# Expert slots cut to narrower widths by rank, with the largest expert in the seventh slot

## The reference

```
gating = x @ router_w.T                       # 1024 x 8
probs = softmax(gating); topk_w, sel = top_k(probs, 2)
h = x @ w1[e].T                               # per expert e: 512 -> 2 x 1024
y = h[..., 1024:] * silu(h[..., :1024])
out = sum over the two chosen experts of topk_w * (y @ w2[e].T)   # 1024 -> 512
```

## Time and profile before

| | before |
|---|---|
| median of three executions | 2489.52 us |
| the profiled execution | 2492.94 us |
| its span | 2491.2 us |
| granted clock of TensorE over the span | 0.978 |
| PE busy in the span | 2365.6 us (95%) |
| DVE, ACT, POOL busy | 51%, 44%, 45% |
| the expert stage | about 2076 to 2491 us |
| DMA in the expert stage | about 155 GB/s |

### The profile page before, as it was taken

How to read it: one execution, slowest core, us unless ns; L and a number is a source line. 1 busy time by engine, 2 the same in 40 slices (tenths; PEclk the granted TensorE clock), 3 DMA queues, 4 the chain that set the end, 5 groups by cost and what they waited for, 6 DMA issues and landing times. The chain is left out here.

```text
span 2491.2 us, 41300 instructions
## 1 busy us (share of the span) xinstructions
PE 2365.6 (95%) x14585; PEld 2088.6 (84%) x14585; DVE 1275.7 (51%) x2146; ACT 1091.7 (44%) x1866; POOL 1119.0 (45%) x470
## 2 busy tenths in 40 slices
PE   8999999999999999999999999999758986999997
PEld 6798989889898988989898898889636756999986
DVE  3255555555555555555555554555755445555542
ACT  3354544445454444445444444444422213444442
POOL 2254555555455555555555555555530014132223
PEclk9999999999999999999999999999979987999999
DMA  4311121211112121211212121111040026465443
GB/s 154 99 48 48 41 60 33 76 41 57 48 41 58 35 76 35 63 48 41 52 41 71 36 66 48 41 48 45 5 161 1 19 81 192 140 168 159 148 146 82
DMA packets 148049, 177.59 MB, mean 71 GB/s; under 512 B 83312, under 2 KB 106736, under 8 KB 147824
## 3 DMA queue, kind: packets, MB, share of 16 engines
q1 hardware_dynamic: 138112, 147.63, 19.9%
q0 software_dynamic: 5104, 10.24, 2.1%
q10 hardware_dynamic: 4608, 16.78, 2.1%
HBM read 135.12 MB, written 39.48 MB: 70 GB/s over the span
## 5 line engine op out<-in xcount | busy, mean ns | idle before, releaser
L395 POOL TENSOR_TENSOR k_parts<-k_t,k_parts 64x1602 fp32r<-64x1602 f32 x128 | 426.1, 3329 | 448.1 <-DVE k_parts L460 448.0
L716 PE MATMUL ps_kv<-ctx_hi,wk_hi 128*128 128x256 f32 (+1 forms) x1536 | 462.5, 301 | 7.6 <-DVE ctx_lo L574 7.6
L716 PE MATMUL ps_kv<-ctx_lo,wk_hi 128*128 128x256 f32 (+1 forms) x1536 | 440.4, 287 | 0.0
L716 PE MATMUL ps_kv<-ctx_hi,wk_lo 128*128 128x256 f32 (+1 forms) x1536 | 440.3, 287 | 0.0
L409 POOL TENSOR_TENSOR v_parts<-v,v_parts 128x832 fp32r<-128x832 f32 x128 | 283.2, 2213 | 335.6 <-ACT v_parts L643 334.1
L506 DVE TENSOR_TENSOR probs_t<-ps_pt,probs_t 128x512 fp32r<-128x512 f32 x368 | 205.8, 559 | 443.8 <-ACT probs_t L625 439.9
L716 PE MATMUL ps_kv<-wv_hi,ctx_hi 128*128 128x512 f32 (+1 forms) x832 | 341.5, 410 | 1.9 <-DVE wv_lo L544 1.9
L716 PE MATMUL ps_kv<-wv_hi,ctx_lo 128*128 128x512 f32 (+1 forms) x832 | 328.2, 394 | 0.0
L716 PE MATMUL ps_kv<-wv_lo,ctx_hi 128*128 128x512 f32 (+1 forms) x832 | 327.3, 393 | 0.0
L613 ACT ACTIVATE k_t<-ps_kv,bk_sb 128x256 f32<-128x256 f32 (+1 forms) x384 | 185.8, 484 | 312.3 <-PE ps_kv L716 309.6
L716 PEld LDWEIGHTS ps_kv<-ctx_hi,wk_hi 128*128 128x128 f32 x1536 | 291.3, 190 | 10.5 <-issue 8.7
(11 more groups left out here) (257 smaller groups left out, 4015.0 us busy)
## 6 DMA issues: line engine op xcount, KB each, us to landing
ctx_raw<-ctx_dram SPq DMA_DIRECT2D x81, 512.0 KB, 3.8
w_raw<-w_dram SPq DMA_DIRECT2D x64, 512.0 KB, 3.6
rows_in<-zeros SPq DMA_DIRECT2D x150, 128.0 KB, 3.5
w_raw<-w_dram ACTq DMA_DIRECT2D x32, 512.0 KB, 3.7
ctx_raw<-ctx_dram SPq DMA_DIRECT2D x16, 644.0 KB, 5.5
q_blocks<-q_parts SPq DMA_DIRECT2D x256, 32.0 KB, 2.0
rows<-rows_in SPq DMA_DIRECT2D x8, 768.0 KB, 4.7
q_parts<-probs_t SPq DMA_DIRECT2D x16, 256.0 KB, 2.0
```

The lines of the kernel that those rows point to most:

```text
L395: nc.gpsimd.tensor_tensor(k_parts[64 - 64 * s:128 - 64 * s, :], k_t[par][64 * s:64 * s + 64, g, :], k_parts[64 * s:64 * s + 64, :].bitcast ...
L716: last = nc.tensor.matmul(o, still, moving, start=(k == 0 and i == 0), stop=(k == DT - 1 and i == 2))
```

## The change

The widths by rank become 384, 320, 320, 288, 288, 256, 192 and 128. Slots are also put in another order: slots 0 to 5 hold ranks 1 to 6, slot 6 holds rank 0 (384 rows), and the last slot rank 7 (128 rows). A width is no longer a bound that always holds: rows past a slot's width go to overflow slots, whose number is counted anew (`most_extra` gives 6, so there are again three passes of the loop). Tiles are cut to the rows that are computed: a slot of 320 rows has tiles of 128, 128 and 64 rows, one of 288 has 128, 128 and 32, one of 256 two of 128, one of 192 has 128 and 64, and the last one a single tile. The counters that engines wait on count these tiles. The rows of a slot are still loaded and transposed as 384.

```diff
-WIDTH = [min(BLOCK, -(-(2 * NT // (k + 1)) // 2) * 2) for k in range(E)]
-LAST_RB = -(-WIDTH[-1] // P)
+WIDTH = [320, 320, 288, 288, 256, 192, BLOCK, 128]
+RANK_OF_SLOT = [1, 2, 3, 4, 5, 6, 0, 7]
+def tile_rows(s):
+    width = WIDTH[s] if isinstance(s, int) else BLOCK
+    return [min(P, width - r * P) for r in range(-(-width // P))]
+def tiles_before(s):
+    if isinstance(s, int):
+        return sum(len(tile_rows(k)) for k in range(s))
+    return s * RB - sum(RB - len(tile_rows(k)) for k in range(E - 1))
...
 def add_rows(s, par, tiles):
-                for r in range(tiles):
+                for r, m in enumerate(tiles):
                     nc.gpsimd.indirect_dma_start(
-                        out=out, out_offset=bass.IndirectOffsetOnAxis(ap=slot_slips[par][:, r, 0:1], axis=0),
-                        in_=down[:, r, :], in_offset=None, compute_op=ALU.add).then_inc(added, 16)
+                        out=out, out_offset=bass.IndirectOffsetOnAxis(ap=slot_slips[par][0:m, r, 0:1], axis=0),
+                        in_=down[0:m, r, :], in_offset=None, compute_op=ALU.add).then_inc(added, 16)
...
 def weigh_down(s, par, tiles):
                 if positive(s):
-                    act.wait_ge(added, 16 * RB * s)
+                    act.wait_ge(added, tiles_before(s) * 16)
...
 def down_part(s, k, tiles):
-                for r in range(tiles):
-                    yh, yl = (part[:, k, r * P:(r + 1) * P] for part in (y_hi, y_lo))
+                for r, m in enumerate(tiles):
+                    yh, yl = (part[:, k, r * P:r * P + m] for part in (y_hi, y_lo))
                     for i, (still, moving) in enumerate([(yh, w2_hi), (yh, w2_lo), (yl, w2_hi)]):
-                        last = nc.tensor.matmul(ps_d[r][:], still, moving[:, k, :], start=(k == 0 and i == 0),
+                        last = nc.tensor.matmul(ps_d[r][0:m, :], still, moving[:, k, :], start=(k == 0 and i == 0),
...
 def slot_tables():
                 then(nc.vector.tensor_reduce(rank_of[:], pairwise[:], AX.X, ALU.add))
+                then(nc.vector.tensor_scalar(lead[:], rank_of[:], 0.0, float(E - 1), ALU.is_equal, ALU.mult))
+                then(nc.vector.scalar_tensor_tensor(out=lead[:], in0=rank_of[:], scalar=-1.0, in1=lead[:],
+                                                    op0=ALU.add, op1=ALU.add))
+                then(nc.vector.tensor_scalar(beyond[:], rank_of[:], float(E - 1), None, ALU.is_equal))
+                then(nc.vector.tensor_tensor(rank_of[:], lead[:], beyond[:], ALU.add))
...
+                then(nc.vector.tensor_tensor(pairwise[:], by_row(rank_of[:]), by_lane(slot_no[:]), ALU.is_equal))
+                then(nc.vector.tensor_tensor(pairwise[:], pairwise[:], by_lane(width_row[:]), ALU.mult))
+                then(nc.vector.tensor_reduce(width_of[:], pairwise[:], AX.X, ALU.add))
+                then(nc.vector.tensor_tensor(beyond[:], counts[:], width_of[:], ALU.subtract))
...
+                then(nc.vector.tensor_tensor(skip[:], skip[:], width_of[:, 1:E], ALU.add))
+                then(nc.vector.tensor_tensor(skip[:], skip[:], width_of[:, 0:E - 1], ALU.subtract))
```

More of the change, by code:

```diff
@@ L7 @@
 from contextlib import ExitStack
+from itertools import product as combinations
 import concourse.bass as bass
@@ L42, with most_extra @@
 RB = BLOCK // P
-WIDTH = [min(BLOCK, -(-(2 * NT // (k + 1)) // 2) * 2) for k in range(E)]
-LAST_RB = -(-WIDTH[-1] // P)
-PAIRS_MAX = (2 * NT // (BLOCK + 1) + 1) // 2
-EXTRA = 2 * PAIRS_MAX + 1
+WIDTH = [320, 320, 288, 288, 256, 192, BLOCK, 128]
+RANK_OF_SLOT = [1, 2, 3, 4, 5, 6, 0, 7]
+def most_extra():
+    by_rank = [WIDTH[RANK_OF_SLOT.index(rank)] for rank in range(E)]
+    most = 0
+    for extra in combinations(range(REGION_BLOCKS), repeat=E):
+        least = [by_rank[rank] + BLOCK * (n - 1) + 1 if n else 0 for rank, n in enumerate(extra)]
+        if sum(max(least[rank:]) for rank in range(E)) <= 2 * NT and max(least) <= NT:
+            most = max(most, sum(extra))
+    return most
+def tile_rows(s):
[5 more added lines that the diff above has]
+    return s * RB - sum(RB - len(tile_rows(k)) for k in range(E - 1))
+LAST_TILES = tile_rows(E - 1)
 ZERO_W = 256
@@ L1072, in attend_route_and_experts @@
         pairwise = sb("pairwise", [P, E, E])
+        lead = sb("lead", [P, E])
+        width_row = sb("width_row", [P, E])
+        width_of = sb("width_of", [P, E])
+        beyond = sb("beyond", [P, E])
         sorted_f = sb("sorted_f", [P, E])
@@ L1256, in add_rows @@
             def add_rows(s, par, tiles):
-                pool.wait_ge(down_free, RB * s + tiles)
+                pool.wait_ge(down_free, tiles_before(s) + len(tiles))
                 if is_first(s):
@@ L1288, in _ @@
             nc.gpsimd.iota(token[:], pattern=[[P, TT], [0, 2]], base=0, channel_multiplier=1).then_inc(pool_consts, 1)
-            pool.wait_ge(pool_consts, 8)
+            for k in range(E):
+                nc.gpsimd.memset(width_row[:, k:k + 1], float(WIDTH[k])).then_inc(pool_consts, 1)
+            pool.wait_ge(pool_consts, 8 + E)
             nc.gpsimd.affine_select(out=triangle[:], in_=all_ones[:], compare_op=ALU.is_gt, fill=0.0, base=0,
@@ L1306, in _ @@
             last = over_slots(pool, slot)
-            add_rows(last, 1, LAST_RB)
-            pool.wait_ge(added, 16 * (RB * last + LAST_RB))
+            add_rows(last, 1, LAST_TILES)
+            pool.wait_ge(added, (tiles_before(last) + len(LAST_TILES)) * 16)
         @block.scalar
@@ L1352, in weigh_down @@
                 if positive(s):
-                    act.wait_ge(added, 16 * RB * s)
-                for r in range(tiles):
-                    nc.scalar.activation(down[:, r, :], ps_d[r][:], ACT.Copy, scale=slot_slips[par][:, r, 1:2].bitcast(F32)
-                                         ).then_inc(down_free, 1)
+                    act.wait_ge(added, tiles_before(s) * 16)
+                for r, m in enumerate(tiles):
+                    nc.scalar.activation(down[0:m, r, :], ps_d[r][0:m, :], ACT.Copy,
+                                         scale=slot_slips[par][0:m, r, 1:2].bitcast(F32)).then_inc(down_free, 1)
             def slot(s, par, last, width):
@@ L1388, in slot @@
                 if not first:
-                    weigh_down(s - 1, 1 - par, RB)
+                    weigh_down(s - 1, 1 - par, tile_rows(s - 1))
             for n in range(NF):
@@ L1429, in _ @@
             split_w2(end_slot, NW2 - 1)
-            weigh_down(end_slot, 1, LAST_RB)
+            weigh_down(end_slot, 1, LAST_TILES)
         @block.vector
@@ L1507, in slot_tables @@
                 then(nc.vector.tensor_reduce(extra_row, past[:], AX.X, ALU.add))
-                then(nc.vector.tensor_scalar(extra_row, extra_row, float(BLOCK), None, ALU.add))
+                then(nc.vector.tensor_scalar(extra_row, extra_row, width_of[:, 0:1], None, ALU.add))
                 then(nc.vector.scalar_tensor_tensor(out=extra_row, in0=some, scalar=float(BLOCK), in1=extra_row,
```

24 lines of the change are left out of this document (13 added, 11 removed).

## The result

| | before | after | ratio |
|---|---|---|---|
| median | 2490.22 us | 2466.99 us (2464.85 to 2467.75) | 0.9905 [0.9888, 0.9923] |
| span of the profiled execution | 2491.2 us | 2465.9 us | |
| granted clock over the span | 0.978 | 0.972 | |

The kernel is faster by 23 us; 47 were forecast. The direction was right, the size was half.

A forecast was written before the change was run, and what follows sets the result against it. PE's matmuls were taken to bound the slots, adds the end. Slots 1 to last -43.0 us, slot 0 -1.5 and the end -2.5 make -47.0: median 2442.5 us, own range 2435 to 2452, with rival 1 2430 to 2509.

The forecast's parts named there:

- the other work fits under it: Shortened slots: DVE's work (at most 26.7 us) and DMA (share 0.74) fit even in the smallest slot, 35.5 us.
- the prediction's own sign: Failure test: the prediction is wrong if the slots' sum misses 300 us by over 10, or slot 0 grows.
- Rival 3: Slots 4, 5 and last: another engine or DMA takes over, 13.6 us more, giving 2456 us; chance 0.06.
- The last slot: Up to the end of slot 6's down product: 41.9 us as before, with 128 columns priced like 256.
- What bounds the end is the adds both times: After slot 6's down product: a chain of adds sets the end; one tile less saves 2.5 us.
- All to 2480.39 stays: At the end: slot 6 keeps three tiles, so everything up to its last add landing at 2480.39 us is unchanged.
- the two prices of a unit: In each slot: up priced by columns (384: 4.18 us, 256: 2.88), down by tiles of the slot before (0.69 us each).
- The estimate of 2.56: Narrow ups (192, 128 columns): 24 weight loads of 0.107 us make 2.56 us, putting the forecast 5 us lower.
- The eight narrow records of the earlier trace: Products moving only 2 columns, read as eight starting 0.10 us apart, taken as the price of loading alone.
- Slot 0: First slot: narrower ups against later tables and POOL work, net -1.5 us, from +2 to -6.5.
- Rivals 1 and 2: Narrow matmuls in slots 5 and last: slower by the column, 2507 us, chance 0.22; or columns alone count, 2427 us, 0.07.
- Rival 4: Rows overflow a slot's width: a pair of overflow slots runs, +103 us, 2546 us; chance 0.03.

The follow-up runs named there:

- experiment 1: Changed kernel with the slips-load wait one slot less again in slots 0 to 6 and at the end (also written `e1_wait_back`); 2451.15 us, ratio 0.9827.
- e11_full_adds: experiment 1, but ACT weighs and POOL adds all 128 rows of every tile, cut ones too; 2447.26 us, ratio 0.9816.
- e1_again: The same kernel as experiment 1, run again beside other kernels; 2448.65 us, ratio 0.9833.
- experiment 9: experiment 1 with 272 in place of 288 columns in slot 2, so one expert overflows and a pair of overflow slots runs; 2541.82 us.
- e5_narrower: experiment 1 with 128 columns in slot 5 and 64 in the last slot, tables unchanged, so rows behind these columns are left out; 2442.54 us.

## Why the prediction was right and wrong

**Failed: the wait of `load_slips` was not priced.** The part on the total says "the other work fits under it". It counts the work of each engine and the bytes, and by both there was room: in the changed kernel DVE is busy for 131 of 249 us and DMA at a share of 0.55. It didn't ask what stands in SP's row ahead of each load, or that the diff makes one of these wait for an event that comes at a fixed distance behind a slot's start. The diff's `positive(s - 1)` became `positive(s)`; I read it as part of the new counting of tiles. It was worth 15.8 of the 16.1 us that slots 2 to 5 miss: so much shorter they are in experiment 1. By the prediction's own sign, a slots' sum more than 10 us off 300, it failed: slots 1 to last took 318.3 us. Rival 3 named the place (short slots) and the victims (PE waiting for DVE, ACT and DMA), but as a lack of bandwidth, with a chance of 0.06, and with 13.6 us for slots 4, 5 and last. The last slot shows nothing of it, and slots 2 and 3 do.

**Part of it is the clock.** In slot 5 PE waits for 6.1 + 0.5 us, yet the slot is 7.0 us over the forecast, although its up is cheaper than forecast (below). Behind the wait the unit's up takes 3.86 us at first, then 2.66. The timeline of PE, and the stages 2329 to 2334 and 2334 to 2344 us:

```profile
2330.19 0.41 PE L1738 MATMUL ps_pair<-rows_lo,w_hi 128*128 128x192 f32 x1
2330.40 0.41 PE L1738 MATMUL ps_pair<-rows_hi,w_lo 128*128 128x192 f32 x1
```

```profile
2329.00:2334.00 5.00, 4.89 (x29) 4.89 (x30) 1.46 (x3) 0.00 (x0) 0.00 (x0) 0.64 0.41 142
...
2334.00:2344.00 10.00, 9.49 (x69) 8.51 (x69) 7.41 (x9) 5.39 (x10) 2.47 (x1) 1.00 0.57 185
```

The matmuls start 0.21 us apart in place of 0.11. PE had stood for 6 us; the granted clock is 0.64 over the next 5 us (part of it at the level of 1.2 GHz), and 1.00 in the 10 us behind. By the two durations of an up this is 1.2 us. Slot 4 has the same behind its 3.8 us: its next up takes 4.19 us, the one after 2.96.

**The last slot: right by two errors.** 42.7 us for 41.9. From its third unit on an up takes 2.63 us, 0.25 less than priced. But its first unit takes 9.1 us where it took 7.3 before, with PE at 1.2 GHz throughout. The stages of the first unit, changed kernel and before, and PE's timeline in the first:

```profile
2395.00:2404.00 9.00, 9.00 (x33) 8.23 (x34) 3.28 (x4) 3.73 (x5) 4.17 (x3) 0.50 0.18 61
```

```profile
2423.00:2430.40 7.40, 7.33 (x34) 6.96 (x35) 2.21 (x3) 3.40 (x5) 3.54 (x3) 0.65 0.25 76
```

```profile
2398.05 0.41 PE L1738 MATMUL ps_pair<-rows_hi,w_lo 128*128 128x128 f32 x1
2398.26 0.41 PE L1738 MATMUL ps_pair<-rows_hi,w_hi 128*128 128x128 f32 x1
```

At this level 64, 128, 192 and 256 columns all start 0.21 us apart, so a narrow width gives back nothing there.

**The end failed too, twice.** "What bounds the end is the adds both times" left out that SP now loads the last slips only when the adds of slot 6 have landed, and ACT waits for that load. The timelines of ACT, of the changed kernel and of experiment 1:

```profile
2458.08 0.69 ACT L1390 ACTIVATE down<-ps_one,slot_slips 128x512 f32<-128x512 f32 x1 [17.18 <-DMA slot_slips<-slips]
```

```profile
2441.71 0.69 ACT L1393 ACTIVATE down<-ps_one,slot_slips 128x512 f32<-128x512 f32 x1 [14.72 <-DMA out_dram<-down,slot_slips]
```

This is 2.6 us (28.2 against 25.6). "All to 2480.39 stays" failed by POOL's pause, some 2.5 us net: the end takes 23.1 us in `e11_full_adds`, where the pause lies elsewhere, close to the 23.6 forecast.

**Right: the two prices of a unit.** Up by columns: 320 took 3.52 us (3.50 forecast), 288 3.16 (3.16), 256 2.87 (2.88), 384 4.18. The narrow ones took 2.66 and 2.63 for 2.88, since the price was that of the nearest row. The estimate of 2.56 by the rule of the Trainium skill (TensorE: Matmul & The Clock Gate, LDWEIGHTS) is nearer; at the 1.2 GHz level that rule doesn't hold, where loads of 128 columns stand 0.21 us apart. The eight narrow records of the earlier trace rows that I took for eight products are four (line 1783 loops over four pieces), with two records each; their distance of 0.10 us stands. Tiles of 64 and 32 rows cost like full ones: the nine matmuls behind an up take 2.07 us with a tile of 64 rows (experiment 1, slot 2), 2.08 with one of 32 (slot 4) and 2.08 with full ones. The records say the same (changed kernel, groups of instructions; busy us, mean ns):

```profile
L1752 PE MATMUL ps_one<-w_hi,y_hi 128*32 128x512 f32 x16 | 6.3, 392 | 0.0
...
L1752 PE MATMUL ps_one<-w_hi,y_hi 128*64 128x512 f32 x24 | 9.4, 394 | 0.0
...
L1752 PE MATMUL ps_one<-w_hi,y_lo 128*128 128x512 f32 x120 | 47.7, 397 | 0.0
```

With the old wait slots 1 to last sum to 301.8 us for the 300.6 forecast. The total of experiment 1 is nevertheless 41 to 43 us under before, not 47: its end is 2.0 us longer than forecast, its slots 1.2, and in its profiled execution slot 0 took 45.7 us for 43.7.

**Slot 0: the number came out by luck.** 43.4 us after, 43.7 forecast. But the same kernel took 45.7 us in `e1_wait_back` and 42.1 in `e1_again`, and the changed kernel with all that were built on it lie from 42.1 to 46.4. In the longer of the two PE stands once with nothing in the profile that ends it:

```profile
2095.92 0.61 PE L1741 MATMUL ps_pair<-rows_hi,w_hi 128*128 128x320 f32 x1 [6.32 <-issue]
```

So one profiled execution can't show a change of 1.5 us here, and the reasons that I gave for it are neither shown nor refuted. What the 6.3 us are stays open.

**Rivals.** Rivals 1 and 2 are refuted by the 0.11 us, and by the slots' sum of 301.8 us with the old wait. Rival 4 didn't happen with these inputs, and experiment 9 puts a price to it.

## What to carry to other kernels

When work gets shorter, look through the rows of the DMA queues for waits, not only at busy shares: a wait at a fixed distance behind a stage's start is free while the stage is long, and becomes a stall of everything behind it in that row once the stage is short. Read each changed index of a wait as an event and ask when that event lands. The wait should name the oldest event that makes the buffer free (experiment 1). Putting the load behind those that needn't wait is another way, which no run here tried.

The best version here that keeps the overflow is the changed kernel with the old wait (0.983 of before, where the change as made has 0.9905).

## What the runs showed of the hardware

- fp32r matmuls start 0.11 us apart for 64, 128 and 192 columns, 0.120 for 256, 0.132 for 288, 0.147 for 320, 0.174 for 384 and 0.231 for 512 columns, at the level of 2.4 GHz. At the level of 1.2 GHz 64 to 256 columns start 0.21 us apart and 512 columns 0.43 (changed kernel and `e5_narrower`, granted clock 0.50).
- A down matmul of 512 columns costs the same with 32, 64 or 128 stationary columns (2.07 to 2.08 us for nine).
- In the changed kernel and all built on it POOL pauses once for 3.5 to 4.0 us between two indirect DMAs: behind the 17th add with cut tiles, behind the 15th with full ones of the same count. The cause is open.
